# New settings for the list schedule of an attention block: a longer allowance for the key copies, and the choices that go with it

## The reference

```python
mod = (_silu(c) @ wmod)                        # shifts, scales and gates
h = layernorm(x) * (1 + ca) + sa
qkv = einsum('bse,ehd->bshd', h, w_qkv)        # S = 2048, E = 128, H = 16, 3 * D = 192
q, k, v = split(qkv, 3)
logits = einsum('bqhd,bkhd->bhqk', q, k) / 8, masked causally
out = einsum('bhqk,bkhd->bqhd', softmax(logits), v)
x = x + ga * einsum('bshd,hde->bse', out, w_out)
h = layernorm(x) * (1 + cb) + sb
x = x + gb * ffn(h)                            # 8 experts, each token goes to its best one
```

## Time and profile before

| | before |
|---|---|
| median of 3 runs (lowest, highest) | 1015.03 us (1014.58, 1017.8) |
| profiled execution | 1014.77 us |
| its span from first to last instruction | 1012.7 us |
| busy TensorE, VectorE, ScalarE | 947.7, 710.9, 678.3 us |
| granted TensorE clock, mean | 0.978 |

### The profile page before, as it was taken

The page is one execution under the profiler, slowest core; times in us unless marked ns, Lnnn a source line. Parts: engine busy times, 40 slices in busy tenths (PEclk is TensorE's granted clock), DMA queues, the critical chain, the costliest instruction groups (busy, mean ns, idle before and its releaser), DMA issues.

```text
span 1012.7 us, 19075 instructions
## 1 busy us (share of the span) xinstructions
PE 947.7 (94%) x6763; PEld 739.3 (73%) x6763; DVE 710.9 (70%) x2278; ACT 678.3 (67%) x1242; POOL 41.2 (4%) x54
## 2 busy tenths in 40 slices
PE   3899999999999999999999999999999999987097
PEld 2677777777777777877777777776777777767097
DVE  4787658875887668866887478756886688735465
ACT  2877668676776757766867677676776687734075
POOL 0000000000000000000000000000000000000544
PEclk9999999999999999999999999999999999996599
DMA  9320111101210121011110121012101111021220
GB/s 212 64 53 12 27 41 40 33 7 33 64 32 12 28 63 35 10 28 42 38 33 7 34 62 32 11 33 53 42 7 33 32 33 32 7 73 37 61 60 27
DMA packets 53678, 40.03 MB, mean 40 GB/s; under 512 B 16277, under 2 KB 42689, under 8 KB 53584
## 3 DMA queue, kind: packets, MB, share of 16 engines
q1 hardware_dynamic: 52336, 36.69, 14.9%
q0 software_dynamic: 1248, 2.13, 0.7%
HBM read 18.21 MB, written 4.25 MB: 22 GB/s over the span
## 4 chain that ended last, share of the span: by engine, by line
PE 83%; DMA 5%; DVE 5%; issue 3%; POOL 2%; ACT 1%; SPq 1%; POOLq 0%; DVEq 0%
PE ps L684 26%; PE ps L712 22%; PE ps L695 21%; PE ps L663 4%; DMA k_split<-k_split 4%; PE ps L723 3%; PE ps L667 2%; PE ps L790 2%; PE ps L800 2%; POOL x_sorted L622 1%; DVE k_split L982 1%; DVE q_split L978 1%; ACT q_split L848 1%; SPq L541 1%; DMA probs<-in_L_wmod_dram 0%
## 5 line engine op out<-in xcount | busy, mean ns | idle before, releaser
L684 PE MATMUL ps<-k_split,q_split 128*128 128x512 f32 (+2 forms) x1280 | 368.4, 395 | 11.4 <-DMA k_split<-k_split 11.3
L862 ACT ACTIVATE probs<-probs,neg_max 128x128 f32<-128x128 f32 (+15 forms) x256 | 308.4, 1207 | 102.9 <-DVE neg_max L1006 102.0
L695 PE MATMUL ps<-ident,probs 128*128 128x128 f32 x2176 | 307.6, 273 | 0.2
L695 PEld LDWEIGHTS ps<-ident,probs 128*128 128x128 f32 x2176 | 258.7, 140 | 60.5 <-issue 23.0
L870 ACT COPY pT<-ps 128x512 f32<-128x512 f32 (+1 forms) x424 | 228.4, 565 | 107.9 <-PE ps L695 97.9
L999 DVE TENSOR_SCALAR_CACHE_REDUCE probs<-ps 128x512 f32<-128x512 f32 (+1 forms) x384 | 250.5, 667 | 57.5 <-PE ps L684 55.5
L712 PE MATMUL ps<-pT,v_sb 128*64 128x256 f32 (+1 forms) x2304 | 250.8, 370 | 0.0
L684 PEld LDWEIGHTS ps<-k_split,q_split 128*128 128x128 f32 x1280 | 202.9, 190 | 41.0 <-issue 15.7
L712 PEld LDWEIGHTS ps<-pT,v_sb 128*64 128x64 f32 x2304 | 157.9, 137 | 86.2 <-issue 13.3
L1002 DVE CUSTOM_DVE_ANT_0 probs<-ps,causal 128x256 f32<-128x256 f32 (+3 forms) x256 | 130.8, 511 | 21.2 <-PE ps L684 19.1
L1024 DVE COPY pT<-ps 128x512 f32<-128x512 f32 (+1 forms) x152 | 97.7, 645 | 19.5 <-PE ps L695 18.8
(11 more groups left out here) (124 smaller groups left out, 547.1 us busy)
## 6 DMA issues: line engine op xcount, KB each, us to landing
k_split<-k_split SPq DMA_DIRECT2D x64, 256.0 KB, 3.7
rinv_b<-spread_rows SPq DMA_DIRECT2D x128, 64.0 KB, 2.6
spread_rows<-rinv_rows SPq DMA_DIRECT2D x256, 0.5 KB
probs<-in_L_ffn_W_dram SPq DMA_DIRECT2D x1, 2048.0 KB, 8.7
w_pair<-in_L_attn_w_qkv_dram SPq DMA_DIRECT2D x24, 64.0 KB, 3.2
hT<-x_sorted SPq DMA_DIRECT2D x23, 65.5 KB, 2.0
x_sorted<-causal SPq DMA_DIRECT2D x1, 1495.0 KB, 13.2
x_sb<-in_L_attn_x_dram SPq DMA_DIRECT2D x4, 256.0 KB, 5.3
```

What stands on the lines that cost most here:

```text
L684: m = pe.matmul(ps_ring[:, s.bank, 0:w], q_split[r % 2][:, q0:q0 + P], k_split[r % 2][:, part, k0:k0 + w], start=(part == 0), stop=(part = ...
L695: m = pe.transpose(ps_turn[:, n % TURN_BANKS, P * r:P * r + P], probs[:, g % 2, r, j * P:j * P + P], ident[:])
L862: act.activation(row, row, ACT.Exp, bias=neg_max[:, g, r:r + 1], accum_out=row_sum[:, g, r:r + 1]).then_inc(exp_done, 1)
```

## The change

Only constants are changed, and all of them are inputs of the plan. The allowance from the low part of k to usable keys goes from 3600 to 4800 ns. The choices are set anew: a PV run starts at 10 waiting tiles and not 11; scores may lead the turns by 1.5 groups and 24 tiles and not 1.4 and 20; a projection is wanted from three groups ahead of its use on and not one (as a last resort from five on, before three); and the ready times of `take` on ACT, `take` on DVE and `add` on DVE count 400, 2500 and 1000 ns later, where they counted 400 ns earlier, as they are, and as they are. No instruction is added or taken out; the order of instructions on each engine, the bank that each step uses, and which of ACT and DVE takes a tile, come out of the plan.

```diff
@@ -20,13 +20,13 @@
 GROUPS = 8
 CHUNKS = 4
 PT_SLOTS = 12
-PV_BATCH = 11
-SCORE_LEAD = 1.4
-SCORE_TILES = 20.0
-TAKE_ACT = -400.0
-TAKE_DVE = 0.0
-ADD_DVE = 0.0
-PROJ_LEAD = 1
+PV_BATCH = 10
+SCORE_LEAD = 1.5
+SCORE_TILES = 24.0
+TAKE_ACT = 400.0
+TAKE_DVE = 2500.0
+ADD_DVE = 1000.0
+PROJ_LEAD = 3
 WEIGHTS_FIRST = 5
@@ -35,7 +35,7 @@
 
 HOP = 60.0
 DRAIN = 180.0
-DOUBLING = 3600.0
+DOUBLING = 4800.0
 PUT = 3600.0
```

## The result

The changed kernel takes 1033.56 us (median of 4 runs, 1032.04 to 1035.07), the kernel before 1014.81 us beside it: a ratio of 1.0178, 95% interval 1.0151 to 1.0205. It is 1.8% slower, where 0.6% faster was forecast. The profiled execution took 1032.36 us, its span is 1030.4 us against 1012.7.

What follows compares the result with a forecast made beforehand. TensorE was taken to bound the kernel; 6.1 us (seven waits) + 1.0 (another wait) + 0.8 (start) − 1.2 (PV runs) = 6.7 us off 1015.03, given as 1008.5 us. Range 1003.5 to 1015.5 us; the forecast's own 1005 to 1012.

Steps and rivals of the forecast that it cites:

- What bounds the kernel, and what the waits are: Attention loop: TensorE is the bound, busy 693.51 of 700 us; only its idle time and switch costs can be saved.
- the seven waits on chunk 1: Pair boundaries: TensorE's 384-wide scores wait for copies of k, 7.19 us together; 85%, 6.1 us, to be recovered.
- DOUBLING and PROJ_LEAD, 7.1 us of gain: Pair boundaries: longer allowance and wider lead fill waits on k copies, 6.1 plus 1.0 us gained; bounds 0 and 8.2.
- the rival of crowding: Pair boundaries: six projections' low parts hold up row maxima and copies; 2.0 us each, 14 us slower, about 1022; chance 0.10.
- The biases, counted at nothing with ±1 us: VectorE and ScalarE: PSUM copies moved to ScalarE, at most 86 us, stay hidden by TensorE's work; nothing counted, ±1 us.
- PV_BATCH, "from none to one run more per pair": Attention loop: none to one PV run more per pair, 0 to 2.4 us; four runs more taken, 1.2 us lost.
- The price of 0.3 us: TensorE in the attention loop: each switch into and out of a PV run costs 0.3 us.
- The sum: Whole kernel: 6.1 + 1.0 + 0.8 − 1.2 = 6.7 us less than 1015.03, so 1008.3, given as 1008.5.
- The signs to look for: New profile: k_split waits under 4 us, TensorE busy over 698 us, last PV some 7 us earlier, at most nine runs a pair.
- Waits of line 684 on row maxima, or of line 695 on copies out of PSUM: TensorE: new waits of these kinds in place of the k_split waits would prove the prediction wrong; no size given.

## Why the prediction was wrong

- **What bounds the kernel, and what the waits are.** Right. TensorE is the bound, and the seven waits on chunk 1, one per pair, could be removed: they are gone in the kernel after and, in a kernel 1.5% faster than the one before, with a lead of two (0.6 us of waits on k_split are left there).
- **DOUBLING and PROJ_LEAD, 7.1 us of gain.** The waits went as said. The allowance alone gave 3.2 to 3.8 us, since it came with ten PV runs more; beside a lead of two it is worth 0.3%. The wide lead had its bad case, the rival of crowding: 1.75 us a boundary at the scores that wait for low parts, where 2.0 us had been worked out. The other 1.1 us of the 2.9 are a wait for ScalarE's copies, which stays at a lead of one. Crowding needs the biases to come about: with TAKE_ACT at −400 and the same lead there is one such wait of 0.9 us.
- **The biases, counted at nothing with ±1 us.** This is the step that failed. The argument was that ScalarE has idle time for VectorE's copies, so that they would be hidden by TensorE's own work. It has the time (VectorE's share fell from 152 to 94 copies), but not when a copy is due: behind an exponential of 1.8 us three banks fill up, and TensorE's list turns to short PV runs. All three undone make the kernel after 30 us faster (1.0178 against 0.9882 of the kernel before), TAKE_ACT alone 28 us; the two biases of VectorE cost nothing that can be told apart once TAKE_ACT is back (0.9893 and 0.9882). That the bias costs this much is shown by these runs; the way it does so is read from the time line at one place of a pair and from the number of runs.
- **PV_BATCH, "from none to one run more per pair".** Of the size of its own part, perhaps (in the list before, a batch of 10 alone makes 77 runs of 71); but a run's number hangs on all the choices together, and the list after has 38 more, six in each steady pair. At 0.25 to 0.30 us that is 10 to 11 us. The price of 0.3 us was right.
- **The sum** added up separate edits. Of the 18.1 us some 10 to 11 are 38 PV runs at the price read from the traces; the other 7 to 8 us are what is left for waits, of which the profile marks only a growth of 2.5 us. The 11.3 us of copies' waits won are already in this number, eaten by the new ones. By the fit the parts would be 14 and 3.6 us, but its number for the runs holds other stalls too.
- **The signs to look for.** "Waits of line 684 on row maxima, or of line 695 on copies out of PSUM" was named as what would prove it wrong: the second stands in the profile with 4.7 us. The waits on k_split were to fall, and fell, but of the other signs three pointed to a loss: 14 PV runs in a steady pair where nine were the most, TensorE busy for 688.67 us where over 698 were hoped for, and the last PV run of the loop 19 us later where 7 us earlier were said. Busy time gave the direction, but a quarter of the size (0.7% against 2.8% of the matmuls): short PV runs count as busy.

The list schedule's own clock had the direction of the change: it ends at 892.4 us for the constants before and at 916.7 us for those after. It is no safe gauge for small steps: it ends at 897.0 us with TAKE_ACT undone, at 905.9 with the longer allowance alone and at 892.6 with the lead of two, and these kernels were measured 1.1, 0.4 and 1.5% faster than the one before.

## What to carry to other kernels

Constants of a greedy schedule have no price one by one. Each changes the whole list; here one constant is worth 28 us, 10 us or 3 us depending on the others, and 200 ns more of it takes 21 us off again. Cost the list that comes out and not the constants: count its mode switches (PV runs) before it is run, and its waits in the profile behind it.

When an engine is at 99% busy, compare the number of instructions done in a stretch, not its busy time alone: 4967, 4827 and 5041 matmuls in 700 us told the three kernels apart, while busy time said 99, 98 and 100%.

Idle time of 30% on an engine doesn't say that work can be given to it, or put later on it, without harm. In this kernel the copies have to come at once and the exponentials ahead of them take 1.8 us: the longest instruction ahead, against the buffers there are, is the number to look at.

## What was not expected of the hardware

The marked idle time of TensorE is less than what a wait costs. Waits marked with 0.50, 0.80 and 0.95 us (kernel after, 495.13, 496.55 and 584.48) make the step from start to start some 0.64, 0.98 and 1.11 us longer than such a step otherwise takes, and the waits of 1.76 and 2.18 us in the earlier trace rows make it 2.06 and 2.48 us longer. It is nearer to an addition of 0.14 to 0.30 us for each wait than to a factor; the fit's 1.42 us for each marked us comes from many waits of less than 1 us.
